# The experts' split weights as 128x512 planes in DRAM, and the context taken earlier by GpSimd

## The chip, the cores and the metric

One core of a Trainium2 chip runs the whole program. The metric is the device time of one execution in microseconds; the reported figure is the median of the runs. TensorE multiplies matrices, VectorE and ScalarE work on vectors (ScalarE also issues DMAs on a queue of its own, called q10 in the profile), GpSimd is called POOL, and SyncE (SP) issues most DMAs (queue q1). GpSimd's DMAs are queue q0. All queues run on the same 16 DMA engines.

## The reference

Sixteen batches of 256 tokens with 256 features pass through cross attention and a feed-forward layer with one shared expert and two routed ones; each token takes one routed expert.

```python
x = x + xattn(layernorm(x), ctx, ctx, Wq, Wk, Wv, Wo)       # 16 heads of 16
h = layernorm(x)
shared = relu(h @ sw1 + sb1) @ sw2 + sb2                     # 256 -> 1024 -> 256
top1 = argmax(softmax(h @ gate_w.T))                         # 0 or 1
# masked[e] is h where top1 == e, else 0
routed = sum_e(relu(masked[e] @ w1[e] + b1[e]) @ w2[e] + b2[e])
x = x + shared + routed
```

Attention runs over 64-token blocks; a softmax is taken in each pair of blocks, and the results are added up by query block. The sequence of 256 stands in a pattern built for 512, so gathers beyond it repeat the last block.

## The kernel before

The program is a software pipeline over the 16 batches, `iteration(i)`, written once for each engine with semaphores between them; iterations 3 to 14 are a hardware loop. Every float32 product is split: a rounded high part and a low part (the rest) are multiplied as three products, so each operand has a `hi` and a `lo` tile, the high made by ScalarE and the low by VectorE or GpSimd.

In iteration i TensorE does, in this order: the 16 score products of batch i (`scores`, L507) interleaved with units of the feed-forward layer; a transpose of the maxima; the projections of batch i+1 for k and q (`front_project`, L467); the transposed scores (`scores_t`, L522) whose exponentials ScalarE writes to PT (L841); four groups of value products (`values`: num at L540, den at L547); the transpose of routed tokens (`routed_tokens`, L473, input `rowin`); the division, the output projection (L587) and v of the next batch. The feed-forward layer runs in eight units an iteration: units 0 to 3 with the routed expert's weights WR, for 256 tokens of one expert gathered through a queue in DRAM, and units 4 to 7 with the shared expert's weights WS. `ffn_up` makes 256 hidden features of a unit, ScalarE applies the relu (L862), GpSimd makes the low part (`hidden_low`, L1337), and `ffn_down` multiplies by the second weights (L675).

The projected k and q lie in T and have to be laid out again, heads on partitions. SP stores them to DRAM (`bounce`, L309: scratch_k<-T, scratch_q<-T, 512 KB each in runs of 1 KB), and reads them back later with six DMAs each (`spread`, L319 and L325, 128 KB each in runs of 1 KB) once the transposed scores of batch i are done. VectorE waits for both bounces before it writes num to T (`numerators`, L1032), and TensorE's second group of value products waits for that copy. SP's order in an iteration is: shift, bounces, load_tile (rowin), residual x, spread, context and x of batch i+2, store of the output.

ScalarE issues the fetch of the routed expert's split weights (`load_weights`, L876), from iteration 2 on, as two DMAs of 2 MB, after the high parts of k and q and ahead of the exponentials. The source is `wx` in DRAM, written once: in iterations 0 and 1 the raw weights are loaded in 24 pieces of 128x512 and split into WR; GpSimd stores each routed piece (`keep`, L1492, 16 of them, 512 KB each). Both experts lie there with all that belongs to a partition side by side, so a fetched half is one run of 16 KB a partition. In the tail SP fetches eight units of 1 MB from wx (`load_unit`, L368).

GpSimd's order in an iteration is: low parts of units 1, 2, 3, 4, with the reciprocal deviation (rstd) and `context_low` (c_lo = ctx_in - c_hi, L1320) of the next batch behind unit 4; unit 5; the bookkeeping of the token queue; the indirect DMAs for it; low parts of units 6, 7 and 0. c_lo is first read by the k projection of the next batch; c_hi is made by ScalarE at the very start of the iteration.

Of the kernel before, what the change touches and what calls it, by code (L numbers as in the profile page):

```python
# [8 lines left out]
F32 = mybir.dt.float32  # L9
# [5 lines left out]
P = 128  # L15
# [29 lines left out]
RU = HT // 2  # L45
# [3 lines left out]
def unit_no(i, k):  # L49

    return k - RU if type(i) is int and i == 1 else UNITS * (i - 2) + k
# [13 lines left out]
def active(i, k):  # L65
    return type(i) is not int or (i >= LAG if k < RU else i >= 1)
# [15 lines left out]
def present(job, i):  # L82
    if type(i) is not int:
        return True
    if job[0] in NEXT:
        return 0 <= i < LAST
    return i >= {"x2T": 1, "cnt": 1, "rT": 2}.get(job[0], 0)
# [32 lines left out]
def slot_pieces(i, w):  # L120
    return PIECE_SLOTS[i][w] if type(i) is int and i in PIECE_SLOTS else ()


def by_vector(n):
    return n % 2 == 1
# [25 lines left out]
def held(engine, registers, *counts):  # L151

    for register, count in zip(registers, counts):
        if type(count) is not int:
            engine.reg_mov(register, count)
    return [c if type(c) is int else r for r, c in zip(registers, counts)]


def R(ap):

    return ap.bitcast(F32R)
# [7 lines left out]
def xattn_ffn(nc, x, ctxT, wT, wraw, b1, b2, gate_w, ident, indicator, blocksum, spread_pairs, low_part, headsum,  # L169
              before_me, place, out):  # L170
    with ExitStack() as ctx:
        def sb(name, shape, dt=F32):
            return ctx.enter_context(nc.sbuf_tensor(name, shape, dt))
# [4 lines left out]
        sem = {name: ctx.enter_context(nc.semaphore(name)) for name in SEMS}  # L178
# [4 lines left out]
        WS, WR = sb("WS", [P, RU, 2, 2, 512]), sb("WR", [P, RU, 2, 2, 512])  # L183
# [54 lines left out]
        scratch_k = nc.dram_tensor("scratch_k", [2, D, SEQ], F32, kind="Internal").ap()  # L238
        scratch_m = nc.dram_tensor("scratch_m", [2, HEADS * NBLK, SEQ], F32, kind="Internal").ap()
        queue = nc.dram_tensor("queue", [QROWS, ROW], F32, kind="Internal").ap()  # L240
        wx = nc.dram_tensor("wx", [2 * P, RU, 2, 2, 512], F32, kind="Internal").ap()
        out_rows = out.rearrange("n t d -> (n t) d")


# [18 lines left out]
        def routed_piece(n):  # L263

            j = n - SHARED_PIECES
            return j // 4 % 2, j % 4, 1 if j < SHARED_PIECES else 0
# [5 lines left out]
        def low_done(n):  # L272

            return (sem["stage_lo_dve" if by_vector(n) else "stage_lo_pool"],
                    sum(by_vector(m) == by_vector(n) for m in range(n + 1)))
# [11 lines left out]
        def _(sp):  # L287
# [77 lines left out]
                    .then_inc(sem["row_loaded"], 16)  # L365

            def load_unit(w, e, k, done):
                sp.dma_start(w.rearrange("p m q c -> p (m q c)"),  # L368
                             wx[P * e:P * e + P, k].rearrange("p m q c -> p (m q c)")).then_inc(sem[done], 16)

            def iteration(i, more, loads=True):
                shift(i)
# [422 lines left out]
        def _(act):  # L795
# [69 lines left out]
            def load_weights(i):  # L865

                selected, = held(act, act_counts, i - 1)
                act.wait_ge(sem["proj_lo"], 4)
                act.wait_ge(sem["sel_done"], selected)
                if type(i) is int and i == 2:  # L870
                    act.wait_ge(sem["wx_stored"], 16 * (PIECES - SHARED_PIECES))
                expert = act.value_load(control[0:1, 1:2], min_val=0, max_val=1)
                if type(i) is not int or i > 2:
                    act.wait_ge(sem["w2_done"], unit_no(i, RU - 1) + 1)
                for h in range(2):
                    act.dma_start(WR[:, 2 * h:2 * h + 2].rearrange("p k a b c -> p (k a b c)"),  # L876
                                  wx[bass.ds(expert * P, P), 2 * h:2 * h + 2].rearrange("p k a b c -> p (k a b c)")) \
                        .then_inc(sem[f"wr_loaded{h}"], 16)

            def routed_high(i):  # L880
# [6 lines left out]
            def iteration(i, more):  # L887
# [23 lines left out]
                if type(i) is not int or i >= 2:  # L911
                    load_weights(i)
# [45 lines left out]
            i = BATCH  # L958
# [354 lines left out]
        def _(pool):  # L1313
# [4 lines left out]
            def context_low(n):  # L1318
                pool.wait_ge(sem["c_hi"], n + 1)
                nc.gpsimd.tensor_tensor(R(c_lo[:, :, :]), ctx_in[:, :, :], c_hi[:, :, :], ALU.subtract) \  # L1320
                    .then_inc(sem["c_lo"], 1)

            def reciprocal_deviation(i, which):

                pool.wait_ge(sem[f"ln{which + 1}_step"], 2 * i + 2)
                nc.gpsimd.tensor_tensor(veps[:, which, :], mv[:, which, :, 1], eps[:, :], ALU.add) \
                    .then_inc(sem[f"veps{which + 1}_done"], 1)
                pool.wait_ge(sem[f"veps{which + 1}_done"], i + 1)
                nc.gpsimd.tensor_tensor(rstd[:, which, :], veps[:, which, :], power[:, :], ALU.pow) \  # L1329
                    .then_inc(sem[f"rstd{which + 1}_done"], 1)  # L1330

            def hidden_low(i, k):
                if not active(i, k):
                    return
                for a in range(2):
                    pool.wait_ge(sem["relu_done"], 2 * unit_no(i, k) + a + 1)
                    nc.gpsimd.tensor_tensor(R(hl[:, k % 2, a]), h32[:, k % 2, a], hh[:, k % 2, a],  # L1337
                                            ALU.subtract).then_inc(sem["hl_done"], 1)

            def add_bias(b):  # L1340
                pool.wait_ge(sem["x1_done"], b + 1)
                if type(b) is not int or b > 0:
                    pool.wait_ge(sem["out_done"], 16 * b)
                nc.gpsimd.tensor_tensor(x1b[:, :, :], x1[:, :, :], bias2[:, None, :].to_broadcast([P, TT, D]),  # L1344
                                        ALU.add).then_inc(sem["x1b_done"], 1)
# [126 lines left out]
            def load(n):  # L1472

                if n >= STAGES:
                    pool.wait_ge(*low_done(n - STAGES))
                    if SHARED_PIECES <= n - STAGES < 2 * SHARED_PIECES:
                        pool.wait_ge(sem["c_step"], 2 * (n - STAGES - SHARED_PIECES) + 2)
                pool.dma_start(stages[:, n % STAGES], wraw[n]).then_inc(loaded(n)[0], 16)

            def split_low(n):  # L1480
                pool.wait_ge(sem["stage_hi"], n + 1)
                hi, lo = piece(n)
                nc.gpsimd.tensor_tensor(R(lo), stages[:, n % STAGES], hi, ALU.subtract) \
                    .then_inc(sem["stage_lo_pool"], 1)

            def keep(n):

                e, k, which = routed_piece(n)
                pool.wait_ge(sem["stage_hi"], n + 1)
                pool.wait_ge(*low_done(n))  # L1490
                w, m = WR, (n - SHARED_PIECES) % SHARED_PIECES
                pool.dma_start(wx[P * e:P * e + P, k, which].rearrange("p b c -> p (b c)"),  # L1492
                               w[:, m // 2, m % 2].rearrange("p b c -> p (b c)")).then_inc(sem["wx_stored"], 16)

            def slot(i, w):
                for n in slot_pieces(i, w):
                    if not by_vector(n):
                        split_low(n)
                    if n >= SHARED_PIECES:
                        keep(n)  # L1500
                    if n + STAGES < PIECES:
                        load(n + STAGES)

            def iteration(i, more):
                later = present(("x2T", 0), i)
                slot(i, 0)
                if later:
                    reciprocal_deviation(i - 1, 1)
                hidden_low(i, 1)
                slot(i, 1)  # L1510
                if later:
                    add_bias(i - 1)
                hidden_low(i, 2)
                slot(i, 2)
                hidden_low(i, 3)
                slot(i, 3)
                hidden_low(i, 4)
                if more:
                    reciprocal_deviation(i + 1, 0)
                    context_low(i + 1)  # L1520
                slot(i, 4)
                hidden_low(i, 5)
                if later:
                    update(i - 1)
                if type(i) is not int or i >= 2:
                    select(i - 1)
                if later:
                    append(i - 1)
                slot(i, 5)
                if active(i, 0):  # L1530
                    add_routed(i)
                for w in range(6, 9):
                    slot(i, w)
                if type(i) is not int or i >= 2:
                    select_bias(i)
                    token_ids(i)
                slot(i, 9)
                for k in (6, 7):
                    hidden_low(i, k)
                hidden_low(i + 1, 0)  # L1540
# [41 lines left out]
            i = BATCH  # L1582
# [90 lines left out]
```

## Time and profile before

| | |
|---|---|
| median of three runs | 1113.38 us (1103.54 to 1113.55) |
| the profiled execution | 1108.92 us, of which the span is 1107.1 us |
| busy shares | TensorE 81%, VectorE 48%, ScalarE 40%, GpSimd 44% |
| mean granted TensorE clock | 0.905 of full speed |
| DMA | 159.69 MB; q1 77.92 MB, q10 58.72 MB, q0 22.61 MB |

The span runs from the first to the last instruction of the profiled execution. Times in the rows are in us from the start of the span. A DMA row in a timeline is the time its issue took on the queue of the issuing engine; the time to landing stands in the DMA view. The share of a queue is the time that its packets took, as a share of 16 engines over the stretch.

### The profile page before, as it was taken

The page shows a single profiled execution, that of the slowest core. Times are in us where ns is not written, and L with a number is a line of the kernel's source. Part 1 is how long each engine was busy: PE and PEld are TensorE (multiplying, and loading weights), DVE is VectorE, ACT ScalarE, POOL GpSimd, SP SyncE. Part 2 cuts the span into 40 slices and gives each one's busy share as a digit, 9 for nine tenths or more (in the row PEclk, how much of TensorE's full clock was granted, in tenths as well). Part 3 has the DMA queues.
Part 4 walks back from the last instruction along what each step waited for, and adds up shares of the span by engine and source line. Part 5 has one row for each costly group of instructions (what it writes and reads, how often), then busy time and mean ns, then how long its engine had stood idle before and what let it go on. Part 6 is the DMA issues. An engine that isn't in the chain of part 4 may idle for free.

```text
span 1107.1 us, 22039 instructions
## 1 busy us (share of the span) xinstructions
PE 894.2 (81%) x7751; PEld 739.1 (67%) x7751; DVE 534.3 (48%) x1090; ACT 447.6 (40%) x991; POOL 489.7 (44%) x798
## 2 busy tenths in 40 slices
PE   3477889988699696969969696987969698889897
PEld 2244667868577484948758494875849486677797
DVE  5657373746356381735537172653817264354300
ACT  3142524454435243443524343452434345244453
POOL 5443424464626254362625346262534526154453
PEclk8586888999999898998989898998989899899999
DMA  8675547566662817566381746548173664714800
GB/s 227 173 243 136 173 94 240 76 233 91 214 109 100 189 40 243 72 233 89 117 183 46 236 63 237 85 143 170 38 235 59 237 85 167 127 49 173 323 11 10
DMA packets 90481, 159.69 MB, mean 144 GB/s; under 512 B 8448, under 2 KB 80512, under 8 KB 85840
## 3 DMA queue, kind: packets, MB, share of 16 engines
q1 hardware_dynamic: 76432, 77.92, 34.2%
q10 hardware_dynamic: 4032, 58.72, 13.3%
q0 software_dynamic: 9984, 22.61, 7.1%
q8 instruction: 20, 0.33, 0.1%
q14 instruction: 13, 0.11, 0.0%
HBM read 119.84 MB, written 39.38 MB: 144 GB/s over the span
## 4 chain that ended last, share of the span: by engine, by line
PE 40%; DMA 22%; issue 12%; POOL 11%; DVE 10%; ACT 3%; SPq 1%; POOLq 0%; DVEq 0%; ACTq 0%
DMA scratch_q<-T 15%; PE acc L675 10%; PE hid L467 8%; POOL hl L1337 6%; PE num L540 5%; PE den L547 4%; PE work L467 3%; PE work L522 2%; PE work L587 2%; DVE nmax L1026 2%; POOL rstd L1329 2%; DMA rowin<-queue 2%; DMA queue<-rows,pos 2%; PE work L573 2%; POOL x1b L1344 1%
## 5 line engine op out<-in xcount | busy, mean ns | idle before, releaser
L1337 POOL TENSOR_TENSOR hl<-h,hh 128x256 fp32r<-128x256 f32 x272 | 202.1, 759 | 335.0 <-ACT hh L862 335.0
L841 ACT ACTIVATE PT<-work 128x512 f32<-128x512 f32 x256 | 131.2, 614 | 179.7 <-PE work L522 172.5
L1032 DVE COPY T<-num 128x512 f32<-128x512 f32 x64 | 44.2, 691 | 308.9 <-DMA scratch_q<-T 172.5
L1026 DVE TENSOR_REDUCE nmax<-work 128x8 f32<-128x512 f32 x256 | 162.4, 681 | 23.4 <-PE work L507 23.4
L540 PE MATMUL num<-PT,V 128*32 128x256 f32 x1024 | 78.9, 432 | 94.0 <-DVE T L1032 94.0
L522 PE MATMUL work<-QP,KP 128*128 128x256 f32 x512 | 107.1, 328 | 30.3 <-DMA QP<-scratch_m 20.1
L862 ACT ACTIVATE h<-hid,bias 128x256 f32<-128x256 f32 x160 | 78.1, 488 | 115.5 <-PE hid L467 115.5
L522 PEld LDWEIGHTS work<-QP,KP 128*128 128x128 f32 x512 | 76.5, 204 | 69.5 <-ACT PT L841 26.8
L507 PE MATMUL work<-KP,QP 96*128 96x512 f32 x256 | 97.9, 459 | 30.1 <-DMA QP<-scratch_q 17.7
L467 PE MATMUL hid<-XS,WS 128*128 128x256 f32 x768 | 110.5, 296 | 2.7 <-DVE idle L1194 2.7
L540 PEld LDWEIGHTS num<-PT,V 128*32 128x32 f32 x1024 | 28.9, 118 | 122.8 <-DVE T L1032 103.2
L467 PEld LDWEIGHTS hid<-XS,WS 128*128 128x128 f32 x768 | 103.1, 201 | 5.6 <-DVE idle L1194 4.3
L467 PE MATMUL hid<-XR,WR 128*128 128x256 f32 x672 | 90.7, 284 | 0.8 <-issue 0.8
L467 PEld LDWEIGHTS hid<-XR,WR 128*128 128x128 f32 x672 | 86.1, 190 | 3.4 <-issue 1.0
L862 ACT ACTIVATE h<-hid,bias_sel 128x256 f32<-128x256 f32 x112 | 53.3, 476 | 83.5 <-PE hid L467 83.5
L862 ACT ACTIVATE hh<-hid,bias 128x256 fp32r<-128x256 f32 x160 | 78.3, 490 | 0.0
L507 PEld LDWEIGHTS work<-KP,QP 96*128 96x128 f32 x256 | 44.5, 203 | 49.4 <-DVE nmax L1026 25.5
L547 PE MATMUL den<-PT,bsum 128*32 128x256 f32 x1024 | 76.7, 423 | 0.0
L675 PE MATMUL acc<-WS,hh 128*128 128x256 f32 x512 | 73.4, 286 | 0.0
L675 PEld LDWEIGHTS acc<-WR,hh 128*128 128x128 f32 x512 | 67.7, 188 | 4.1 <-DVE x1b L1121 0.2
L675 PEld LDWEIGHTS acc<-WS,hh 128*128 128x128 f32 x512 | 64.2, 188 | 9.3 <-issue 8.8
L675 PE MATMUL acc<-WR,hh 128*128 128x256 f32 x512 | 69.5, 278 | 0.0
(238 smaller groups left out, 1638.8 us busy)
## 6 DMA issues: line engine op xcount, KB each, us to landing
WR<-wx ACTq DMA_DIRECT2D x28, 2048.0 KB, 11.6
KP<-scratch_k SPq DMA_DIRECT2D x96, 128.0 KB, 5.0
QP<-scratch_q SPq DMA_DIRECT2D x96, 128.0 KB, 8.1
scratch_k<-T SPq DMA_DIRECT2D x16, 512.0 KB, 3.3
scratch_q<-T SPq DMA_DIRECT2D x16, 512.0 KB, 15.5
wx<-WR POOLq DMA_DIRECT2D x16, 512.0 KB, 4.2
stages<-wraw POOLq DMA_DIRECT2D x24, 256.0 KB, 4.4
xin<-x SPq DMA_DIRECT2D x16, 256.0 KB, 9.4
```

The lines of the kernel that those rows point to most:

```text
L467: mm = nc.tensor.matmul(dst, R(s), R(m), start=n == 0, stop=n == len(steps) - 1)
L507: nc.tensor.matmul(bank, R(QP[0:SHIFT_ROW, p, P * t:P * t + P]), R(KP[0:SHIFT_ROW, p, :, :]), start=True, stop=True).then_inc(sem["s_full" ...
L522: mm = nc.tensor.matmul(bank[:, SEQ * t:SEQ * t + SEQ], R(KP[:, p, s, P * t:P * t + P]), R(QP[:, p, :]), start=True, stop=True)
L540: mm = nc.tensor.matmul(num[r:r + 32, j, :], V[:, t, 2 * p + s, :], PT[:, (2 * p + s) % 8, t, :], start=True, stop=True)
L547: mm = nc.tensor.matmul(den[r:r + 32, 0, :], bsum[:, p, :], PT[:, (2 * p + s) % 8, t, :], start=p == 0, stop=p == PAIRS - 1, skip_group_ch ...
L573: mm = nc.tensor.matmul(bank[32 * q:32 * q + 32, :, queries], hsum[:, r, :], pairs[:, q, :, queries], start=True, stop=True)
L675: mm = nc.tensor.matmul(acc[:, t, :], R(h[:, k % 2, a, P * t:P * t + P]), R(w2_part(w, part, a)), start=first, stop=last_unit and h is hl ...
L841: nc.scalar.activation(PT[:, j % 8].rearrange("p t q -> p (t q)"), work[:, BANK[("st", j)], :], ACT.Exp).then_inc(sem["exp_done"], 1)
L862: last = nc.scalar.activation(dst, hid[:, k % 2, a, :], ACT.Relu, bias=b[:, a:a + 1])
L1026: nc.vector.tensor_reduce(nmax[:, t, 8 * p:8 * p + 8], work[:, BANK[("s", j)], :].rearrange("q (b k) -> q b k", k=BLOCK), AX_X, ALU.max, n ...
L1032: nc.vector.tensor_copy(T[:, 2 * v:2 * v + 2, :], num[:, :, :]).then_inc(sem["num_copied"], 1)
L1337: nc.gpsimd.tensor_tensor(R(hl[:, k % 2, a]), h32[:, k % 2, a], hh[:, k % 2, a], ALU.subtract).then_inc(sem["hl_done"], 1)
```

## The change

The DRAM tensor wx is laid out as 64 planes of 128x512 values: for each expert, unit, kind (first or second weights) and part (high or low) one plane. The same bytes are stored and fetched by the same DMAs, but each run is now 2 KB: a partition of ScalarE's half fetch has eight runs in place of one of 16 KB, one of a tail unit four in place of one of 8 KB, and one of a store two in place of one of 4 KB. Beside it GpSimd's `context_low(i + 1)` moves from behind the low part of unit 4 (and rstd) to the place between units 2 and 3.

```diff
-        wx = nc.dram_tensor("wx", [2 * P, RU, 2, 2, 512], F32, kind="Internal").ap()
+        wx = nc.dram_tensor("wx", [2 * RU * 4, P, 512], F32, kind="Internal").ap()
...
             def load_unit(w, e, k, done):
-                sp.dma_start(w.rearrange("p m q c -> p (m q c)"),
-                             wx[P * e:P * e + P, k].rearrange("p m q c -> p (m q c)")).then_inc(sem[done], 16)
+                sp.dma_start(w.rearrange("p m q c -> p (m q) c"),
+                             wx[4 * (RU * e + k):4 * (RU * e + k) + 4].rearrange("n p c -> p n c")) \
+                    .then_inc(sem[done], 16)
...
                 for h in range(2):
-                    act.dma_start(WR[:, 2 * h:2 * h + 2].rearrange("p k a b c -> p (k a b c)"),
-                                  wx[bass.ds(expert * P, P), 2 * h:2 * h + 2].rearrange("p k a b c -> p (k a b c)")) \
+                    act.dma_start(WR[:, 2 * h:2 * h + 2].rearrange("p k a b c -> p (k a b) c"),
+                                  wx[bass.ds(expert * 4 * RU + 8 * h, 8)].rearrange("n p c -> p n c")) \
                         .then_inc(sem[f"wr_loaded{h}"], 16)
...
-                pool.dma_start(wx[P * e:P * e + P, k, which].rearrange("p b c -> p (b c)"),
-                               w[:, m // 2, m % 2].rearrange("p b c -> p (b c)")).then_inc(sem["wx_stored"], 16)
+                at = 4 * (RU * e + k) + 2 * which
+                pool.dma_start(wx[at:at + 2].rearrange("n p c -> p n c"), w[:, m // 2, m % 2]) \
+                    .then_inc(sem["wx_stored"], 16)
...
                 hidden_low(i, 2)
                 slot(i, 2)
+                if more:
+                    context_low(i + 1)
                 hidden_low(i, 3)
                 slot(i, 3)
                 hidden_low(i, 4)
                 if more:
                     reciprocal_deviation(i + 1, 0)
-                    context_low(i + 1)
```

## Rows read from the trace of the kernel before

**Rows 1.** The page's costliest groups: busy us, mean ns, idle before and its releasers
```profile
L1032 DVE COPY T<-num 128x512 f32<-128x512 f32 x64 | 44.2, 691 | 308.9 <-DMA scratch_q<-T 172.5
```

**Rows 2.** All waits: engine, line, what it waited for: us in total, times, longest
```profile
DVE T L1032 <- DMA scratch_q<-T: 172.5, 11, 15.9
```

**Rows 3.** Timeline of SP, 735 to 805 us: start, us, line, operation
```profile
738.02 0.38 SPq L309 DMA_DIRECT2D scratch_q<-T  x1
...
760.26 2.70 SPq L319 DMA_DIRECT2D KP<-scratch_k  x6
...
802.32 0.38 SPq L309 DMA_DIRECT2D scratch_q<-T  x1
```

**Rows 4.** Timeline of TensorE, same iteration; in brackets idle before and its releaser
```profile
754.50 1.94 PE L540 MATMUL num<-PT,V 128*32 128x256 f32 x16 [8.63 <-DVE T L1032]
...
765.38 0.60 PE L473 MATMUL work<-id,rowin 128*128 128x128 f32 x4
...
776.37 0.64 PE L507 MATMUL work<-KP,QP 96*128 96x512 f32 x2
```

**Rows 5.** DMA issues in 736 to 800 us, time to landing
```profile
scratch_q<-T SPq DMA_DIRECT2D x1, 512.0 KB, 15.6
```

**Rows 6.** Stretches of 2 us: busy times, then PEclk, DMA share, GB/s
```profile
754.00:756.00 2.00, 1.50 (x16) 0.79 (x20) 0.44 (x1) 0.00 (x0) 1.37 (x3) 0.50 0.34 119
```

**Rows 7.** Timeline of ScalarE (its queue of DMAs), same iteration
```profile
738.14 0.85 ACTq L876 DMA_DIRECT2D WR<-wx  x2
```

**Rows 8.** DMA queues in 740 to 743 us: packets, MB, share of 16 engines
```profile
q10 hardware_dynamic: 66, 1.08, 85.8%
q1 hardware_dynamic: 64, 0.07, 6.1%
```

**Rows 9.** Queues in 735.5:737.5, 5.5:6.5, 762:772 and 737.5:753.5 us, in this order
```profile
q1 hardware_dynamic: 504, 0.51, 85.0%
...
q1 hardware_dynamic: 128, 0.25, 67.8%
...
q1 hardware_dynamic: 1501, 1.37, 114.9%
...
q10 hardware_dynamic: 288, 4.19, 66.0%
```

**Rows 10.** Iteration 3: SP, ScalarE and TensorE timelines, and its q bounce's landing
```profile
232.92 0.38 SPq L309 DMA_DIRECT2D scratch_q<-T  x1
...
289.89 0.38 SPq L309 DMA_DIRECT2D scratch_q<-T  x1
...
233.26 0.85 ACTq L876 DMA_DIRECT2D WR<-wx  x2
...
251.24 0.66 PE L473 MATMUL work<-id,rowin 128*128 128x128 f32 x4 [1.37 <-DMA rowin<-queue]
...
264.02 0.73 PE L507 MATMUL work<-KP,QP 96*128 96x512 f32 x2 [1.57 <-DMA QP<-scratch_q]
...
scratch_q<-T SPq DMA_DIRECT2D x1, 512.0 KB, 4.8
```

**Rows 11.** Timelines of GpSimd and VectorE, 728 to 788 us
```profile
729.35 1.29 POOL L1320 TENSOR_TENSOR c_lo_t<-ctx_in,c_hi_t 128x512 fp32r<-128x512 f32 x1
...
787.57 1.67 POOL L1337 TENSOR_TENSOR hl<-h,hh 128x256 fp32r<-128x256 f32 x2 [2.27 <-ACT hh L862]
...
729.42 1.70 DVE L1003 TENSOR_SCALAR xhat<-xin,mv,rstd 128x256 f32<-128x256 f32 x2 [0.32 <-POOL rstd L1329]
...
778.70 0.73 DVE L1003 TENSOR_SCALAR rows<-x,mv,rstd 128x256 f32<-128x256 f32 x2
```

**Rows 12.** Groups of GpSimd: busy us, mean ns, idle before
```profile
L1492 POOL DMA_DIRECT2D wx<-WR x16 | 9.1, 567 | 19.7 <-DVE WR L1127 13.5 <-POOL WR L1483 4.0 <-ACT WR L831 1.6
```

**Rows 13.** The chain in order of time, tail
```profile
1041.43 7.41 DMA out<-yr,ids
```

**Rows 14.** Iteration 2: SP's timeline
```profile
188.54 5.31 SPq L319 DMA_DIRECT2D KP<-scratch_k  x6
```

## The prediction

> **What bounds the kernel now.** I read the chain of work that ended last first, since no engine is full: TensorE is busy for 81% of the span. Its largest single piece is no engine at all but the DMA that stores the projected queries from T into scratch_q (the "q bounce"): eleven pieces of some 15.6 us, 15% of the span. The table of waits says who is held: VectorE's copy of num into T (L1032) waits for that DMA 11 times, 172.5 us of the 308.9 that it idles in all [rows 1, 2]. These are iterations 4 to 14, and all look alike. I work in the one whose bounce is issued at 738.02 us; the next is issued at 802.32, so a period is 64.30 us [rows 3]. TensorE stands idle for 8.63 us ahead of the second group of value products, until 754.50 [rows 4], since the bounce needs 15.6 us to land [rows 5]. While it idles its granted clock falls to 0.50, that is 1.2 GHz [rows 6], and the sixteen products take 1.94 us [rows 4].
>
> **Why it takes 15.6 us.** ScalarE issues both halves of the routed expert's fetch, 2 MB each in runs of 16 KB, 0.12 us behind the bounce [rows 3, 7]. In the 3 us behind 740 the fetch's queue (q10) moved 66 packets and SP's queue (q1) moved 64 [rows 8]: one packet of each in turn. A 16 KB packet costs an engine 0.660 x 16 us x 16 engines / 256 = 660 ns (32 of the 288 are completions) [rows 9]. A 1 KB packet of a bounce costs 0.85 x 2 x 16 / 494 = 55 ns (some 10 are completions) [rows 9]. Each engine has 16 packets of the fetch and 32 of the bounce. So the bounce gets 16 turns while the fetch takes 16 x 0.66 = 10.6 us, and finishes only behind it. Iteration 3 is a natural experiment: there the fetch came 0.34 us behind the bounce, the bounce was mostly through, and it landed in 4.8 us [rows 10]. That iteration lasted from 232.92 to 289.89, 56.97 us [rows 10].
>
> **The change, first part: the fetch in 2 KB runs.** It removes nothing; 4 MB still move, in 128 packets for each engine. One 2 KB packet costs 0.678 x 1 x 16 / 118 = 92 ns in a stretch of startup loads [rows 9]; the lower bound is an eighth of 660, 83 ns. I take 92: the fetch then costs 11.8 us of each engine instead of 10.6. In turns of 55 + 92 = 147 ns the bounce's 32 packets take 4.7 us; about 0.9 us ahead of the first and 1.1 us of GpSimd's packets and completion make 6.7, so it lands near 744.7. TensorE could start the second group at 754.50 - 8.63 = 745.87, for which the copy (0.69 us [rows 1]) must start by about 745.1. The wait goes.
>
> What is next on TensorE is read from iteration 3. There the token transpose (L473) could have started at 251.24 - 1.37 = 249.87, 16.95 us behind the bounce's issue [rows 10]; in the late iterations it starts 27.36 us behind (765.38 - 738.02) [rows 3, 4]. So 10.4 us are at stake, 8.6 of idle and the rest from work done at the half clock. The period of TensorE alone is 64.3 - 10.4 = 53.9 us.
>
> What is late next is DMA. The spread of q and k (L319, L325), 96 packets an engine, starts when the score products are done: at 760.26 - 738.02 - 10.4, 11.8 us behind the bounce [rows 3]. It runs at 1337 data packets in 10 us, 8.4 an engine and us, 11.5 us in all [rows 9]. The score products of the next iteration start 776.37 - 765.38 = 11.0 us behind the transpose [rows 4], so they want it landed at 16.95 + 11.0 = 27.9 us. If it only takes its turn in a sum, 0.9 + 1.8 (bounce) + 11.8 (fetch) + 3.8 (GpSimd's, rowin, x) + 11.5 + 0.5 = 30.3 us, 2.4 late. Iteration 3 shows this wait at 1.57 us, and one for rowin at 1.37 [rows 10]. If the spread's packets cost 55 ns between packets of the fetch (alone they queue up on each other, a share of 115% at only 1.37 MB in 10 us), it is on time. I take the middle, 1.2 us. Rowin no longer waits behind 16 KB packets: issued some 6 us behind the bounce, its 16 packets of about 0.2 us (one of each queue) land near 11 us, ahead of 16.95; that is an estimate from the same packet costs.
>
> ScalarE issues both fetches ahead of its exponentials. Rows of before show 0.85 us for the two [rows 7]; for eight times the runs I keep that, with 2 us more as the bad end of this case. Ahead of that end lies a rival below.
>
> **Second part: context_low ahead of unit 3.** GpSimd's c_lo (1.29 us) now runs from 729.35 to 730.64, beside VectorE's normalization x-hat, whose two instructions take 1.70 us together [rows 11]; the same pair for rows, with no c_lo beside it, takes 0.73 [rows 11]. All that follows on VectorE up to the projections is on the chain, so moving it gives up to 0.9 us. At its new place GpSimd is idle for 2.27 us ahead of the low part of unit 3 [rows 11], which hides it. There it meets the gate's products on VectorE, which may then lose up to 0.9 us of a busy stretch. Bounds -0.9 to +0.9 us of gain; I take +0.5. Its DMA-side effect is none: ctx_in is read earlier, and the next load of it is asked for much later by SP.
>
> The Trainium skill ("SBUF — State Buffer", section Who interferes with whom) says that VectorE and GpSimd share one port pair under an exclusive lock, so the later one blocks. The trace agrees in the 1.70 us; by that rule alone c_lo would take as much from the gate's products as it gives back to x-hat, and this part would be worth nothing.
>
> **Third: the rest.** The 16 stores of wx by GpSimd cost 567 ns each [rows 12]; as two runs a partition between 0 and 0.5 us more each, 0 to 8 us, most of it beside other work: 2 us. In the tail the add of routed rows takes 7.41 us beside 8 KB packets [rows 13]; with 2 KB ones I expect 3 less, bounds 0 and 4.
>
> **Sum.** 11 x (10.4 - 1.2 + 0.5) = 106.7. Iteration 3 falls from 57.0 to 54.6, and iteration 2, with no row shown, I take alike: 4.8. Tail 3, stores -2. Together 112.5 off the profiled execution's 1108.9 us (span 1107.1), so 996. The median of the runs is 1113.4, 0.4% above it; I leave 996.
>
> **The rivals.**
> *ScalarE is held.* A DMA instruction can be held at issue: in iteration 2, beside the fetch, six issues of SP took 5.31 us, against 2.70 in the iteration at 738 [rows 3, 14]. With 128 packets an engine queued, ScalarE's second issue could wait and delay the exponentials behind it by 2 to 10 us. Against it: those 2.70 us passed while the spread's own queue was deep. Time 1056 to 1108.
> *Slower.* The same place, past its break-even: if the hold is over 9 us, the exponentials, not the bounce, keep TensorE, and more is lost than the 8.6 us idle. The whole fetch drains in 128 x 147 ns = 18.8 us; half way between, 4.5 us a period over 13 periods, gives 1109 + 58 = 1167.
> *Turns by several packets.* If an engine took a group of 2 KB runs as one turn, the bounce would wait as now: 11 x 0.5 gained at most, 1105. The turns of now speak against it [rows 8], though they are of one run a packet on both queues.
> The Trainium skill ("DMA: Bandwidth & Descriptors", section Queues, rings and completion order) states such a rule, whole packets of some 9 to 17 descriptors from one ring before the next; the trace's 66 to 64 does not look like it.
> *It does not do what it says* is covered by that time as well: the stall goes nowhere.
>
> **How the numbers follow.** Main case 0.72. Its best end: 11 x (10.4 + 0.9) + 10 = 134 off, 975. Its worst: 11 x (10.4 - 2.4 - 0.9 - 2) - 4 = 52 off, 1057. ScalarE held 0.12, turns 0.07, slower 0.09. To leave out no more than 0.2 the range must reach into the held case, to 1090. About 1% is what this kernel's runs can tell from no change (they spread over 0.9%). Faster: the main case and most of the held one, 0.82; same 0.08; slower 0.10.
>
> **What would show it.** Right: q10 with eight times the packets at about 90 ns; the bounce landing in 6 to 7 us with the fetch beside it; no wait of L1032 for it; ids of rowin early; TensorE's clock at 1.00 in the value products; periods of 53 to 57 us; a small new wait for QP from scratch_q or for ctx_in; x-hat's pair in under 1 us. Wrong: L876 of several us on ScalarE's queue with PT's exponentials behind it; a bounce still over 12 us; or a wait of over 3 us for QP at the first score product, which would mean that I priced the DMA engines too low.

## The result, and the profile after

The changed kernel takes 1046.62 us (median of 4 runs, 1046.23 to 1051.12) against 1110.26 us for the kernel before on the same chip (1103.54 to 1113.55); the ratio is 0.944, 95% interval 0.939 to 0.950. The forecast was 996 us: the sign was right and the time lies in the range, but a little over half of the forecast gain came. The profiled execution took 1046.23 us with a span of 1044.4 us, so 62.7 us of the forecast 112.5 are there. TensorE's mean granted clock rose from 0.905 to 0.931. In the changed kernel the lines shown here carry numbers 1 or 2 higher than before (L1032 is now L1034, L507 L509, L876 L878).

The page of the changed kernel, its shares, queues, groups and landings:

```profile
PE 892.8 (85%) x7751; PEld 743.6 (71%) x7751; DVE 524.3 (50%) x1090; ACT 446.0 (43%) x991; POOL 489.1 (47%) x798
...
q10 hardware_dynamic: 29120, 58.72, 16.5%
...
PE 39%; issue 20%; POOL 16%; DVE 6%; ACT 5%; DMA 4%; ACTq 2%; POOLq 1%; SPq 0%; DVEq 0%
...
L509 PE MATMUL work<-KP,QP 96*128 96x512 f32 x256 | 104.7, 483 | 61.4 <-DMA QP<-scratch_q 40.7
L1034 DVE COPY T<-num 128x512 f32<-128x512 f32 x64 | 44.2, 690 | 217.0 <-PE num L542 217.0
...
WR<-wx ACTq DMA_DIRECT2D x28, 2048.0 KB, 15.1
...
scratch_q<-T SPq DMA_DIRECT2D x16, 512.0 KB, 3.4
```

Against [rows 1, 2] the copy of num no longer waits for the bounce at all: its 217.0 us of idle are all spent waiting for TensorE's products. The bounce lands in 3.4 us, not 15.6 [rows 5], and not in the 6.7 us of the forecast. What is new is the first score product (L509), which waits 40.7 us for QP from scratch_q. The waits of the changed kernel (in total, times, longest):

```profile
PE work L509 <- DMA QP<-scratch_q: 40.7, 13, 14.8
ACT c_hi_t L827 <- DMA ctx_in<-ctxT: 32.7, 14, 12.6
```

The longest of each lies at the start of the kernel; the rest come once an iteration. One iteration of the changed kernel on SP, ScalarE, TensorE and VectorE in turn (it answers to [rows 3, 4, 7, 11]):

```profile
640.85 0.38 SPq L310 DMA_DIRECT2D scratch_q<-T  x1
...
698.89 0.38 SPq L310 DMA_DIRECT2D scratch_q<-T  x1
```
```profile
641.95 1.13 ACTq L878 DMA_DIRECT2D WR<-wx  x2
643.28 4.03 ACT L843 ACTIVATE PT<-work 128x512 f32<-128x512 f32 x8 [3.17 <-issue]
...
672.52 0.63 ACT L827 ACTIVATE c_hi_t<-ctx_in 128x512 fp32r<-128x512 f32 x1 [1.34 <-DMA ctx_in<-ctxT]
```
```profile
658.69 0.60 PE L475 MATMUL work<-id,rowin 128*128 128x128 f32 x4
...
663.01 1.58 PE L469 MATMUL hid<-XR,WR 128*128 128x256 f32 x12
...
671.85 0.75 PE L509 MATMUL work<-KP,QP 96*128 96x512 f32 x2 [1.90 <-DMA QP<-scratch_q]
672.41 2.74 PE L469 MATMUL hid<-XR,WR 128*128 128x256 f32 x12
```
```profile
682.41 1.38 DVE L1072 CUSTOM_DVE_ANT_0 PT<-rows,gate 128x256 f32<-128x256 f32 x1
...
683.72 0.42 DVE L1072 CUSTOM_DVE_ANT_0 PT<-rows,gate 128x256 f32<-128x256 f32 x1
...
690.85 0.73 DVE L1005 TENSOR_SCALAR xhat<-xin,mv,rstd 128x256 f32<-128x256 f32 x2
```

Three things are to be seen. The period is 698.89 - 640.85 = 58.04 us, where it was 64.30 and forecast 54.6. The token transpose (L475) starts 17.84 us behind the bounce, near the forecast 16.95, but the score products start at 31.00 us, 1.90 us late for QP, and the same kind of twelve products (L469, from WR) that took 1.58 us at 663 take 2.74 us at 672. The stretches of 2 us from 670 say why (PEclk, DMA share and GB/s are the last three numbers; this answers to [rows 6]):

```profile
670.00:672.00 2.00, 0.15 (x1) 0.15 (x2) 0.96 (x5) 1.17 (x2) 0.91 (x2) 1.00 0.99 231
672.00:674.00 2.00, 2.00 (x10) 1.92 (x11) 1.61 (x4) 0.63 (x1) 0.00 (x0) 0.60 0.43 147
674.00:676.00 2.00, 2.00 (x10) 1.81 (x10) 0.69 (x2) 0.58 (x2) 0.00 (x0) 0.54 0.00 0
```

TensorE idled with the DMA engines at 0.99; then the granted clock of two stretches was 0.60 and 0.54, near the 0.50 that is 1.2 GHz. And third: the fetch is issued 641.95 - 640.85 = 1.10 us behind the bounce, where before it came 0.12 us behind [rows 3, 7]. The prediction had not looked for that. It comes from the other part of the change: x-hat's pair takes 0.73 us instead of 1.70 [rows 11] and all that follows up to the bounce moves about 1 us ahead, but ScalarE's fetch waits for the chosen expert (`control`, written by GpSimd), which did not get earlier. Both can be counted from TensorE's product of the token mask, first before, then in the changed kernel:

```profile
728.16 0.18 PE L602 MATMUL work<-mask,tri 128*128 128x2 bf16 x1
...
737.18 0.18 POOL L1422 CAST control<-taken 128x2 int32<-128x2 f32 x1
```
```profile
689.99 0.18 PE L604 MATMUL work<-mask,tri 128*128 128x2 bf16 x1
...
699.01 0.18 POOL L1424 CAST control<-taken 128x2 int32<-128x2 f32 x1
```

The choice comes 9.02 us behind the mask in both. The bounce comes 738.02 - 728.16 = 9.86 us behind it before and 698.89 - 689.99 = 8.90 us now.

**Where the 62.7 us are.** From the bounce rows of both timelines: the ten periods between the bounces of iterations 4 and 14 fell from (930.35 - 289.89) / 10 = 64.05 to (874.64 - 293.24) / 10 = 58.14 us, 59.1 us in all; iterations 2 and 3 together became 2.6 us longer (iteration 2 is 1.0 us shorter, iteration 3 is 3.6 us longer); all ahead of them 0.8 us longer; what follows the last bounce went from 1107.1 - 930.35 = 176.8 to 1044.4 - 874.64 = 169.8, 7.0 less. 59.1 - 2.6 - 0.8 + 7.0 = 62.7.

So two theories stood against each other. The first is the prediction's: the 2 KB runs free the bounce from its wait. The second: the 1.1 us that the context's move puts between bounce and fetch frees it, and the 2 KB runs cost time.

### The profile page after: what moved, and what is told of

Read it like the earlier page. It is cut to its first block, busy times and chain, and to the rows that moved or that the text cites. A ratio compares the mean times of both kernels' runs of the same rounds, so it can differ in the third digit from the quotient of the medians.

```text
span 1044.4 us, 22039 instructions
## 1 busy us (share of the span) xinstructions
PE 892.8 (85%) x7751; PEld 743.6 (71%) x7751; DVE 524.3 (50%) x1090; ACT 446.0 (43%) x991; POOL 489.1 (47%) x798
## 4 chain that ended last, share of the span: by engine, by line
PE 39%; issue 20%; POOL 16%; DVE 6%; ACT 5%; DMA 4%; ACTq 2%; POOLq 1%; SPq 0%; DVEq 0%
PE acc L677 9%; PE hid L469 8%; POOL hl L1339 7%; PE num L542 5%; PE den L549 4%; PE work L524 4%; ACT PT L843 3%; PE work L589 2%; PE work L575 2%; POOL rstd L1331 2%; POOL c_lo_t L1322 1%; POOL x1b L1346 1%; ACTq L878 1%; DVE nmax L1028 1%; DMA rowin<-queue 1%
## 5 line engine op out<-in xcount | busy, mean ns | idle before, releaser
L1339 POOL TENSOR_TENSOR hl<-h,hh 128x256 fp32r<-128x256 f32 x272 | 199.9, 750 | 277.5 <-ACT hh L864 277.3
L509 PE MATMUL work<-KP,QP 96*128 96x512 f32 x256 | 104.7, 483 | 61.4 <-DMA QP<-scratch_q 40.7
L1034 DVE COPY T<-num 128x512 f32<-128x512 f32 x64 | 44.2, 690 | 217.0 <-PE num L542 217.0
L524 PEld LDWEIGHTS work<-QP,KP 128*128 128x128 f32 x512 | 73.6, 195 | 82.6 <-ACT PT L843 45.3
L469 PE MATMUL hid<-XS,WS 128*128 128x256 f32 x768 | 109.1, 293 | 1.1 <-DVE idle L1196 1.1
L509 PEld LDWEIGHTS work<-KP,QP 96*128 96x128 f32 x256 | 47.0, 210 | 86.9 <-DVE nmax L1028 36.6
L469 PEld LDWEIGHTS hid<-XS,WS 128*128 128x128 f32 x768 | 101.6, 199 | 3.5 <-DVE idle L1196 2.7
L469 PE MATMUL hid<-XR,WR 128*128 128x256 f32 x672 | 95.6, 294 | 0.8 <-issue 0.8
L469 PEld LDWEIGHTS hid<-XR,WR 128*128 128x128 f32 x672 | 91.1, 201 | 3.6 <-issue 1.0
L542 PE MATMUL num<-PT,V 128*32 128x256 f32 x1024 | 74.3, 411 | 1.6 <-DVE T L1034 1.6
L677 PEld LDWEIGHTS acc<-WR,hh 128*128 128x128 f32 x512 | 70.0, 194 | 4.6 <-DVE x1b L1123 0.2
L549 PE MATMUL den<-PT,bsum 128*32 128x256 f32 x1024 | 70.2, 394 | 0.0
L985 DVE SCALAR_TENSOR_TENSOR a_lo_t<-work,a_hi_t 128x512 fp32r<-128x512 f32 x33 | 22.8, 691 | 76.1 <-ACT a_hi_t L802 73.5
```

Source lines behind the costliest of these rows:

```text
L469: mm = nc.tensor.matmul(dst, R(s), R(m), start=n == 0, stop=n == len(steps) - 1)
L509: nc.tensor.matmul(bank, R(QP[0:SHIFT_ROW, p, P * t:P * t + P]), R(KP[0:SHIFT_ROW, p, :, :]), start=True, stop=True).then_inc(sem["s_full" ...
L524: mm = nc.tensor.matmul(bank[:, SEQ * t:SEQ * t + SEQ], R(KP[:, p, s, P * t:P * t + P]), R(QP[:, p, :]), start=True, stop=True)
L542: mm = nc.tensor.matmul(num[r:r + 32, j, :], V[:, t, 2 * p + s, :], PT[:, (2 * p + s) % 8, t, :], start=True, stop=True)
L549: mm = nc.tensor.matmul(den[r:r + 32, 0, :], bsum[:, p, :], PT[:, (2 * p + s) % 8, t, :], start=p == 0, stop=p == PAIRS - 1, skip_group_ch ...
L677: mm = nc.tensor.matmul(acc[:, t, :], R(h[:, k % 2, a, P * t:P * t + P]), R(w2_part(w, part, a)), start=first, stop=last_unit and h is hl ...
```

## The experiments

The kernel before was run beside each group, and every ratio is against it: 1115.74 us beside e1 to e4, 1111.06 us beside e5 to e8, 1105.57 us beside e9. Where kernels of different groups are set against each other in microseconds, about 1% of the difference may not be theirs; the ratios are free of that.

**Each part alone.** e1_planes_only is the changed kernel with `context_low` back at its old place. e2_context_only is the kernel before with only that move:

```diff
                 slot(i, 2)
+                if more:
+                    context_low(i + 1)
                 hidden_low(i, 3)
...
                     reciprocal_deviation(i + 1, 0)
-                    context_low(i + 1)
```

> Only the 128x512 planes; the context stays behind unit 4, so the fetch should again be issued about 0.1 us behind the q bounce. Theory A (turns of one packet on each engine, so 2 KB packets free the bounce by themselves): the bounce lands in 6 to 8 us with the fetch beside it, no wait of VectorE for it, time 1045 to 1060. Theory B (what freed the bounce in the changed kernel is that the fetch came 1.1 us later, because the context's new place made the projections earlier than the expert's choice; the planes matter little): the bounce still lands in 12 to 16 us and the time is 1095 to 1112.

> Only the context ahead of unit 3; the fetch keeps its 16 KB runs. Theory A: the bounce is held behind 16 KB packets as before, time 1095 or more. Theory B: the fetch is issued about 1.1 us behind the bounce, by then the bounce is mostly through and lands in 3.4 to 5 us; time 1045 to 1060, with rowin later and a wait for it as in iteration 3 of the kernel before.

The planes alone: 1072.35 us, ratio 0.960 (0.952 to 0.968). The context alone: **1006.62 us**, ratio 0.903 (0.897 to 0.908), 40 us faster than the change as a whole, with ScalarE's fetch 1.09 to 1.15 us behind the bounce again. Neither kernel met a time that was written down for it: the planes alone are slower than the band of theory A (1045 to 1060 us), and the context alone is far faster than that of theory B (1045 to 1060 us), and without the wait for rowin expected there. One of its iterations (SP, ScalarE, TensorE; then landings and queues in 615 to 671 us):

```profile
616.43 0.38 SPq L309 DMA_DIRECT2D scratch_q<-T  x1
...
671.03 0.38 SPq L309 DMA_DIRECT2D scratch_q<-T  x1
```
```profile
617.57 0.85 ACTq L876 DMA_DIRECT2D WR<-wx  x2
```
```profile
634.02 0.60 PE L473 MATMUL work<-id,rowin 128*128 128x128 f32 x4
...
645.61 0.73 PE L507 MATMUL work<-KP,QP 96*128 96x512 f32 x2 [0.43 <-DMA QP<-scratch_q]
```
```profile
q10 hardware_dynamic: 288, 4.19, 18.9%
...
WR<-wx ACTq DMA_DIRECT2D x2, 2048.0 KB, 11.0
...
scratch_q<-T SPq DMA_DIRECT2D x1, 512.0 KB, 3.4
```

The period is 54.60 us, and with runs of 16 KB the bounce lands in 3.4 us. The token transpose starts 17.59 us behind it, the score products 29.18 us, 1.82 us sooner than in the changed kernel. The fetch costs each engine 0.189 x 56 = 10.6 us. The same view of the changed kernel, 639 to 697 us:

```profile
q10 hardware_dynamic: 2080, 4.19, 21.2%
...
WR<-wx ACTq DMA_DIRECT2D x2, 2048.0 KB, 14.9
```

That is 0.212 x 58 = 12.3 us an engine (96 ns a packet), 1.7 us more, and the score products start 1.8 us later than in e2. In e1_planes_only (the fetch 0.10 to 0.19 us behind the bounce in the loop; this distance is called the lead below) the bounce is let through after all: VectorE waits for it 3 times in the whole run, once 6.09 us in the iteration at 658, and there TensorE waits 4.25 us for QP:

```profile
DVE T L1034 <- DMA scratch_q<-T: 18.4, 3, 6.3
```
```profile
690.71 1.22 PE L509 MATMUL work<-KP,QP 96*128 96x512 f32 x2 [4.25 <-DMA QP<-scratch_q]
```

**The table of two by two.** If the lead frees the bounce in e2_context_only, taking the lead away must bring the stall back. e5_context_no_lead (e2 as base) and e9_planes_no_lead (the changed kernel as base) make SP wait for ScalarE's conditions before it issues the bounce of q:

```diff
+                if type(n) is not int or n >= 3:
+                    chosen, = held(sp, sp_counts, n - 2)
+                    sp.wait_ge(sem["ident_loaded"], 16)
+                    sp.wait_ge(sem["q_lo"], n + 1)
+                    sp.wait_ge(sem["sel_done"], chosen)
+                    sp.value_load(control[0:1, 1:2], min_val=0, max_val=1)
```

> The context-only kernel (16 KB runs, 1007 us) with one added wait: SP stores q only when the expert has been chosen, and reads the choice as ScalarE does, so that the bounce and the fetch are issued within some 0.2 us again; the bounce itself goes out about 1 us later. Theory B (the lead of the bounce over the fetch is what freed it): the stall of 15 us is back in every period, time 1085 to 1110. Theory E (the context's new place saves time in other ways, the lead is incidental): 1 us a period lost, 1010 to 1025.

> The changed kernel with both of its edits, but with the fetch no longer behind the bounce: SyncE waits for the expert's choice before it issues the bounce, so both are issued within 0.2 us of each other (1.1 us apart in the changed kernel). It fills the last cell of a table of two by two: 16 KB runs with a lead of 1.1 us 1006.6 us, 16 KB runs without a lead 1137.7 us, 2 KB runs with a lead 1046.6 us. Theory T (the queues take turns packet by packet, so 2 KB runs free the bounce by themselves): the bounce lands in 6 to 8 us instead of some 15, the second projections begin some 3 us later than in the changed kernel, and part of that is hidden by the fetch's own 15 us; 1055 to 1085 us. Theory O (the order of issue alone frees the bounce, whatever the length of a run): the bounce lands in 13 us or more and the time is 1110 to 1140 us. The planes with the context at its old place gave 1072.3 us at a lead of 0.1 to 0.2 us, which speaks for T, but there the xhat passes were late too.

The fetch then goes out 0.06 and 0.05 us ahead of the bounce, and the bounce itself 10.0 us behind the mask's product, where in e2 it was 8.9. The bounce's landing, in a window of one iteration, first in e5, then in e9:

```profile
scratch_q<-T SPq DMA_DIRECT2D x1, 512.0 KB, 16.2
```
```profile
scratch_q<-T SPq DMA_DIRECT2D x1, 512.0 KB, 6.5
```

| | lead 1.1 us | no lead |
|---|---|---|
| runs of 16 KB | 1006.6 us (e2), period 54.9, bounce 3.4 us | 1137.7 us (e5), period 65.2, bounce 16.2 us |
| runs of 2 KB | 1046.6 us (the change), period 58.1, bounce 3.4 us | 1054.7 us (e9), period 59.3, bounce 6.5 us |

(Periods are means from the bounce of iteration 4 to that of 14. Ratio to before: e5 1.024, 1.022 to 1.026; e9 0.952, 0.944 to 0.959.) With the fetch first the planes are worth 83 us; at a lead of 1.1 us they cost 40. With 16 KB runs the lead is worth 131 us, with 2 KB runs 8, and that 8 isn't clear of noise: the intervals of the two ratios overlap (0.939 to 0.950 and 0.944 to 0.959). e5 missed its expected time on the slow side. TensorE's stall is back there, and in two iterations more than before (13 waits against 11 [rows 2]):

```profile
DVE T L1038 <- DMA scratch_q<-T: 226.1, 13, 17.7
```
```profile
517.04 1.94 PE L546 MATMUL num<-PT,V 128*32 128x256 f32 x16 [9.30 <-DVE T L1038]
```

In the kernel before, the fetch of iterations 2 and 3 went out 0.52 and 0.34 us behind the bounce and neither stalled; in e5 they stall too and take 129.4 us together instead of 114.6. That is half of the 28 us between the two spans. The rest is 1.2 us a period in the loop. So 83 and 131 us are worth more than the stall of the kernel before: at its own leads (0.06 to 0.18 us in the loop) the planes alone take off 43 us (e1).

e9 settles that the turns of one packet, as the prediction read them from 66 against 64, hold for 2 KB runs too: the bounce lands in 6.5 us against the 6.7 worked out, and in the 3 us from 529.5, with both under way, the two queues moved as many packets each:

```profile
q10 hardware_dynamic: 267, 0.55, 74.7%
q1 hardware_dynamic: 268, 0.27, 28.8%
```

VectorE waits there for the bounce 12 times, 94.0 us in all, but TensorE doesn't: in the iteration with the bounce at 527.96 its second group of value products starts with no idle time in brackets, 7.9 us behind (in [rows 4] 8.63 us of idle stood there).

```profile
535.87 1.07 PE L548 MATMUL num<-PT,V 128*32 128x256 f32 x16
```

Its time is slightly under the expected band; that wait is nearly all hidden. With the same planes, and without a lead in either, e9 and e1 differ by the context move: 59.3 against 60.1 us a period, ratios 0.952 and 0.960 with overlapping intervals.

**Is it DMA work?** e7_after_half_fetch is the changed kernel with the second half of the fetch cut to one plane of eight; it leaves seven of the eight planes of units 2 and 3 unfetched, whichever expert was chosen, so it computes less than the others. e8_context_4k_runs has planes of 128x1024, runs of 4 KB, and the context ahead of unit 3:

```diff
-                for h in range(2):
-                    act.dma_start(WR[:, 2 * h:2 * h + 2].rearrange("p k a b c -> p (k a b) c"),
-                                  wx[bass.ds(expert * 4 * RU + 8 * h, 8)].rearrange("n p c -> p n c")) \
...
+                act.dma_start(WR[:, 2, 0, 0:1],
+                              wx[bass.ds(expert * 4 * RU + 8, 1)].rearrange("n p c -> p n c")) \
+                    .then_inc(sem["wr_loaded1"], 16)
```
```diff
-        wx = nc.dram_tensor("wx", [2 * RU * 4, P, 512], F32, kind="Internal").ap()
+        wx = nc.dram_tensor("wx", [2 * RU * 2, P, 1024], F32, kind="Internal").ap()
```

> The changed kernel; the second half of each fetch moves one plane of eight (units 2 and 3 of the routed expert keep old weights), so 56 packets an engine fewer, about 5.4 us of engine work. Theory D (DMA work up to the landed spread bounds the period): the waits for QP and ctx_in go, the periods fall from 58 to about 54.5 and the time to 990 to 1005. If the 2 KB runs cost through something else (ScalarE held, the stores of wx), the time stays above 1030.

> The changed kernel with planes of 128x1024, so runs of 4 KB; context ahead of unit 3. Theory F (each packet costs a fixed 13 ns or so on top of its bytes: 96 ns for 2 KB against 661 for 16 KB): 64 packets x 172 ns, 11.0 us a fetch against 10.6 and 12.3, so 1012 to 1020. Theory G (short runs harm the other queues by taking more turns, whatever they cost themselves): halfway or worse, 1025 to 1040.

e7: 998.98 us, ratio 0.899 (0.898 to 0.901), inside its expected 990 to 1005. The waits of e7 for QP, the start's 14.7 us alone:

```profile
PE work L509 <- DMA QP<-scratch_q: 14.7, 1, 14.7
```

e8: 1023.44 us, ratio 0.921 (0.920 to 0.923), between the two times expected and in neither. Its fetch in a window of 64 us:

```profile
q10 hardware_dynamic: 1056, 4.19, 17.8%
```

That is 178 ns a packet, 11.4 us an engine. In order of the fetch's cost an engine, at the same lead: 7.4 us (e7, 0.132 x 56) period 54.7; 10.6 us (16 KB) 54.9; 11.4 us (4 KB) 56.2; 12.3 us (2 KB) 58.1. Between 7.4 and 10.6 us the fetch costs next to nothing; from there each further microsecond adds about 1.9 to the period, since the late score products bring the idle time and then the half clock. That it is the engine time of the fetch that costs, and not the number of turns that it takes between the packets of the spread (16, 64 and 128 an engine), isn't shown: over 16, 4 and 2 KB runs the time rises in line with either, and e7 has fewer packets and less engine time.

**The time of the fetch.** Three kernels move the fetch without touching GpSimd. e3_before_late_fetch and e4_after_late_fetch put `load_weights` behind the first group of exponentials (four instructions), in the kernel before and in the changed one; e6_context_exp_first puts it behind the first exponential alone in e2. The edit of e3 and e4 is:

```diff
-                if type(i) is not int or i >= 2:
-                    load_weights(i)
...
+                if type(i) is not int or i >= 2:
+                    load_weights(i)
```

> The kernel before with one edit: ScalarE issues the fetch behind the first four exponentials instead of ahead of them, some 3 us later. Layout and context as before. Both theories give a free bounce (3.4 us). If the bounce's wait was all that cost, the period falls by 7 to 10 us and the time is 1020 to 1050; if DMA is the next bound, the later fetch makes the spread of q and k land later and the time stays at 1050 to 1070.

> The changed kernel with the fetch behind the first four exponentials. Theory C (in the changed kernel ScalarE's wait for the expert's choice ahead of the exponentials costs 1.3 us a period on the path): 1046 - 13 x 1.3 = 1030. Theory D (the DMA engines' work between the bounce and the landed spread is the bound, so what TensorE gains there it waits for at the first score product): 1044 to 1050.

> The context-only kernel with the fetch issued behind the first exponential of a batch instead of ahead of it. ScalarE stands idle 2.9 us ahead of that exponential, of which the wait for the expert's choice is about 1.2 us. Theory C (this wait is on the path): 13 x 1.0 less, about 993. Theory D (DMA work from bounce to spread is the bound): 1003 to 1009, with more wait at the first score product.

e3: 1032.29 us, ratio 0.925 (0.920 to 0.930), with a lead of 3.1 to 3.4 us, 16 KB runs and the context where it was. The later place of the fetch alone is worth 83 us against the runs of before beside it. Its period is 56.7 us, 7.4 less than before. e4: 1067.96 us, ratio 0.959 (0.952 to 0.966) against the changed kernel's 0.944, slower than both times expected: with 2 KB runs a later fetch only brings QP later (40.7 us of this wait in the changed kernel).

```profile
PE work L509 <- DMA QP<-scratch_q: 48.7, 13, 13.7
```

So ScalarE's wait for the expert ahead of its exponentials, 3 us in the changed kernel, was not what held it. e6 shows this more cleanly: its first exponential no longer waits for the choice (ScalarE's idle time ahead of the exponentials put down to issue falls from 41.9 us in e2 to 18.8), and the fetch still goes out 1.12 to 1.15 us behind the bounce from iteration 4 on, as in e2. It takes 1009.30 us, ratio 0.908 (0.906 to 0.909), no better than e2 and at the edge of the 1003 to 1009 expected. Why e3, with the bounce free and 16 KB runs, stays 26 us behind e2 is only argued: its QP waits (25.3 us) are near e2's (22.4), but the transpose of tokens waits for rowin 12 times, 10.2 us, and its x-hat pass is still beside c_lo. No kernel here separates these.

## Why the prediction came out as it did

The period falls into five legs, from one iteration of each kernel (the bounces at 738.02, 616.43 and 640.85):

| us | before | e2 | changed kernel |
|---|---|---|---|
| bounce to token transpose | 27.36 | 17.59 | 17.84 |
| transpose to first scores | 10.99 | 11.59 | 13.16 |
| first scores to third pair | 3.73 | 3.82 | 5.36 |
| third pair to mask product | 12.36 | 12.74 | 12.78 |
| mask product to next bounce | 9.86 | 8.86 | 8.90 |
| period | 64.30 | 54.60 | 58.04 |

The score products ahead of the mask, in the fourth leg, before and in the changed kernel:

```profile
790.14 1.10 PE L507 MATMUL work<-KP,QP 96*128 96x512 f32 x2
```
```profile
687.68 1.09 PE L509 MATMUL work<-KP,QP 96*128 96x512 f32 x2 [0.41 <-DVE nmax L1028]
```

- **What bounds the kernel, and what the stall is worth: right.** Of the 10.4 us at stake e2 gets 9.8, in the first leg, and its mean period of 54.9 is near the 54.6 forecast: 64.05 - 54.91 = 9.1 us less against 9.7.
- **Turns of one packet, bounce in 6.7 us: right** (e9, 6.5 us, 267 packets against 268), and the rival of turns by several packets is out. The Trainium skill ("DMA: Bandwidth & Descriptors", section Queues, rings and completion order) has whole packets of several descriptors from one ring before the next; the counts in e9 don't look like it, and e9 and e1 show the bounce let through between 2 KB runs. But in the changed kernel this mechanism has almost nothing left to do: some 8 us, within the noise.
- **Context move at +0.5 us a period: right as time on the chain, and the step that failed most, for its effect on DMA.** The last leg gains 0.96 us, since x-hat is faster. The fourth loses 0.4, since the gate's products are slower and TensorE now waits for a maximum of the scores. That is 0.5 us net, the forecast. What failed is that it was counted only as time on the chain. What it does to the order of two DMA issues 0.12 us apart was written off ("Its DMA-side effect is none"), though iteration 3, with the fetch 0.34 us behind, stood among the rows as a natural experiment. The move alone takes 109 us off the runs of before beside it. The Trainium skill ("SBUF — State Buffer", section Who interferes with whom) has VectorE and GpSimd share one port pair under a lock, and the trace agrees: x-hat's mean is 409 ns against 908 over its 32 instructions, and the gate's product beside c_lo takes 1.38 us where the next takes 0.42. Yet "worth nothing", which the prediction drew from that rule, did not follow: of what the gate's products lose, only 0.4 us is on the chain.
- **Fetch at 92 ns a packet and DMA 1.2 us late: mis-sized, and this is most of what kept the time from 996.** It was 96 ns a packet (12.3 us against 11.8) and 1.90 us of wait, inside the bound of 2.4. But behind that wait the half clock makes twelve products take 2.74 us instead of 1.58 and the next pair of score products 1.03 instead of 0.63, which the sum left out, though it had counted the half clock in the stall of before. 58.04 against 54.60 us in e2 is 3.4 us: 1.8 from the later start of the scores and 1.5 from this (third leg). In the ten periods of the loop (58.14 against 54.91 us) that is 32 of the missing 50 us.
- **Rowin near 11 us: wrong, without effect.** It is issued 651.69 - 640.85 = 10.8 us behind the bounce, not 6, and lands 6.4 us later, in time for the transpose at 17.8.
- **Iterations 2 and 3, +4.8: wrong.** They had no stall to lose and got the longer fetch: 2.6 us lost. With 16 KB runs (e2) they gained 3.3.
- **Tail +3: wrong size.** The last add of routed rows takes 7.00 us against 7.41 [rows 13].
- **Stores -2: about right.** They take 745 ns each against 567 [rows 12], 16 x 0.18 = 2.8 us of issue; all that lies ahead of iteration 2's bounce, the stores with it, became 0.8 us longer.
- **ScalarE held: out.** The two issues take 1.13 us against 0.85 [rows 7], and e6 shows that time there isn't on the path.

That the time lay in the range was partly luck: the part that was rated at 5% of the gain brings 109 us alone, more than the whole, and the part that was rated highest brings 43 us alone but costs 40 beside the other. The version that beats both kernels is e2_context_only, 1006.62 us (before 1115.74 beside it).

## What to carry to other kernels

Where a small urgent store and a long fetch go out on two queues within a few tenths of a microsecond, list the lead of one over the other in every iteration before pricing an edit; anything that shifts either side changes which is served first, and that was worth over 100 us here. Shorter runs protect the small transfer in either order tried here, but every iteration pays for them in DMA time; where the order can be had, keep the long runs and get the order. Test an edit of two parts as a table of two by two, since the planes' value here changes its sign with the lead, and that of the context move falls from 109 us to some 26 beside the planes.

## What was not expected of the hardware

- With 16 KB runs in the other queue, a 512 KB store of 1 KB runs lands in 3.4 us with a lead of 1.1 us and in 16.2 us without (e2, e5); with 2 KB runs in 3.4 and 6.5 us (the change, e9).
- The stall comes and goes within half a microsecond of lead: with the same 16 KB runs iterations 2 and 3 of the kernel before, at 0.52 and 0.34 us, don't wait for the bounce, and all eleven at 0.06 to 0.18 us do.
- After 1.90 us of idle TensorE worked some 4 us at a granted clock of 0.60 and 0.54; after e2's 0.43 us it stayed at 1.00.
- A packet of the fetch beside other queues costs 661 ns at 16 KB (0.189 x 56 x 16 / 256), 178 ns at 4 KB and 96 ns at 2 KB: 10.6, 11.4 and 12.3 us an engine for the same 4 MB. In startup loads a 2 KB packet had cost 92 ns [rows 9].
- ScalarE's issues of 1024 runs each cost 0.57 us against 0.43 for 128.
